# Linear attention: VectorE copies the second sweep's corner ahead of the sum of the keys' squares

## What is computed

```python
x = x + _L0_attn_ref(_layernorm(x), ...)
x = x + _L0_ffn_ref(_layernorm(x), ...)
x = x + _L1_attn_ref(_layernorm(x), ...)     # the gated delta rule
x = x + _L1_ffn_ref(_layernorm(x), ...)
```

```python
q = _l2norm(q) * Dk ** (-0.5); k = _l2norm(k)        # x * rsqrt(sum(x * x) + eps)
attn = -(einsum('bhcid,bhcjd->bhcij', k_beta, k) * decay_mask)   # strictly lower triangle
# rows corrected one after the other: the inverse of a unit triangular matrix
value_corrected = attn @ v_beta
...
out = inter + einsum('bhij,bhjd->bhid', intra, v_prime)
new_state = state * gel_c[..., None] + einsum('bhld,bhle->bhde', k_c * kd_c, v_prime)
```

## Time and profile before

| | us |
|---|---|
| median of 3 runs | 1651.46 |
| lowest and highest | 1650.98, 1653.03 |
| the profiled execution, its own time | 1658.11 |
| its span, first to last instruction | 1656.3 |
| first run of the loop with a next head, start of its ksum | 549.50 |
| last such run, start of its ksum | 1406.87 |
| TensorE busy over the span | 1406.0 (85%) |
| VectorE busy over the span | 1159.5 (70%) |

### The profile page before, as it was taken

The page is one execution under the profiler, slowest core; times in us unless marked ns, Lnnn a source line. Parts: engine busy times, 40 slices in busy tenths (PEclk is TensorE's granted clock), DMA queues, the critical chain, the costliest instruction groups (busy, mean ns, idle before and its releaser), DMA issues. The chain is left out here.

```text
span 1656.3 us, 38451 instructions
## 1 busy us (share of the span) xinstructions
PE 1406.0 (85%) x14366; PEld 1000.5 (60%) x14366; DVE 1159.5 (70%) x2384; ACT 827.7 (50%) x2173; POOL 784.9 (47%) x1112
## 2 busy tenths in 40 slices
PE   5987995596555989999999999999999999976575
PEld 2443344464423657677777777777777777764464
DVE  5888117573566787888888888888888888833623
ACT  2333982224033655666665665666666666632122
POOL 5101001487024366457567566566566656633443
PEclk9998998699776999999999999999999999977787
DMA  8200005282724454564654664655556556331883
GB/s 278 85 2 2 1 1 155 89 249 107 251 51 98 109 146 114 149 158 127 161 158 129 150 154 140 146 155 148 141 152 156 130 151 171 89 91 58 247 253 130
DMA packets 249433, 218.72 MB, mean 132 GB/s; under 512 B 88770, under 2 KB 224962, under 8 KB 247200
## 3 DMA queue, kind: packets, MB, share of 16 engines
q1 hardware_dynamic: 234992, 192.41, 43.1%
q0 software_dynamic: 5712, 15.60, 2.8%
q10 hardware_dynamic: 8544, 8.26, 1.6%
HBM read 133.85 MB, written 82.25 MB: 130 GB/s over the span
## 5 line engine op out<-in xcount | busy, mean ns | idle before, releaser
L1974 DVE SCALAR_TENSOR_TENSOR d_conv<-d_big,all_cw,d_conv 128x1023 f32<-128x1023 f32 (+2 forms) x192 | 245.3, 1278 | 46.2 <-ACT d_conv L2216 44.3
L1696 PE MATMUL d_big<-all_xn_t,all_w 128*128 128x512 f32 x512 | 251.8, 622 | 18.6 <-DVE d_conv L1974 11.8
L1696 PEld LDWEIGHTS d_big<-all_xn_t,all_w 128*128 128x128 f32 x512 | 93.7, 198 | 102.3 <-issue 89.0
L2450 POOL TENSOR_TENSOR d_y<-d_y,all_xn 128x256 f32<-128x256 f32 x128 | 97.8, 764 | 110.2 <-DVE d_y L2126 92.1
L2315 ACT COPY d_ys<-d_big 128x128 f32<-128x128 f32 x256 | 60.9, 266 | 178.3 <-PE d_big L1864 140.7
L1902 PE MATMUL d_big<-all_wo,d_yt 128*128 128x256 f32 x512 | 125.9, 391 | 13.8 <-DVE d_yt L2051 13.8
L1835 PE MATMUL d_big<-all_w,all_xn_t 128*128 128x256 f32 x512 | 124.3, 387 | 0.0
L2407 POOL TENSOR_TENSOR d_vs<-d_vs,d_sv 128x1024 f32<-128x1024 f32 x32 | 61.3, 1915 | 131.3 <-DMA d_vs<-turned_v_scratch 130.0
L1902 PEld LDWEIGHTS d_big<-all_wo,d_yt 128*128 128x128 f32 x512 | 97.1, 197 | 26.5 <-issue 14.3
L1835 PEld LDWEIGHTS d_big<-all_w,all_xn_t 128*128 128x128 f32 x512 | 94.5, 192 | 19.8 <-issue 8.8
L2025 DVE SCALAR_TENSOR_TENSOR d_AI<-d_big,d_b_col,d_decay 128x256 f32<-128x256 f32 x256 | 104.3, 474 | 1.4 <-PE d_big L1709 0.6
(11 more groups left out here) (451 smaller groups left out, 3552.8 us busy)
## 6 DMA issues: line engine op xcount, KB each, us to landing
turned_kq_scratch<-d_turned SPq DMA_DIRECT2D x32, 512.0 KB, 3.8
d_kq_tok<-turned_kq_scratch SPq DMA_DIRECT2D x128, 128.0 KB, 3.0
turned_v_scratch<-d_vs SPq DMA_DIRECT2D x16, 1024.0 KB, 4.1
d_vs<-turned_v_scratch SPq DMA_DIRECT2D x64, 256.0 KB, 5.6
grouped_y_scratch<-d_yx SPq DMA_DIRECT2D x32, 512.0 KB, 3.4
d_yx<-grouped_y_scratch SPq DMA_DIRECT2D x128, 128.0 KB, 3.2
all_w<-in_L_attn_W_qkvz SPq DMA_DIRECT2D x16, 768.0 KB
l_hold<-in_L_ffn_gate_up_proj SPq DMA_DIRECT2D x48, 192.0 KB, 3.3
```

The source lines that it names most:

```text
L1696: mm = pe.matmul(big[0][:, c, :], w_sb[par][:, k, n * DK:(n + 1) * DK], xn_t[:, k, c * 512:(c + 1) * 512], start=(k == 0), stop=(k == KD - 1))
L1974: dve.scalar_tensor_tensor(conv[:, sh:T], src[:, 0:T - sh], cw[:, bass.ds(g, 1), COLUMN_OF[j], 3 - sh], conv[:, sh:T], ALU.mult, ALU.add). ...
L2450: pool.tensor_tensor(part, part, zs[:, t, :], ALU.mult).then_inc(s["yg_s"], 1)
```

## The change

In VectorE's list of steps, `ksum` of the next head moves from ahead of `l1y` of this head to right behind it. Nothing else changes: the same instructions, the same waits, the same buffers. The first head's `ksum`, ahead of the loop, stays where it is.

```diff
@@ -1366,7 +1366,7 @@
 DVE_ORDER = steps_of("""
...
-    3; this l1p, l0x 2; next kq_turn 1; prev y_turn 0; next ksum; this l1y; next kb; this l2p; next products 0, products 1; this l2y; next products 2;
+    3; this l1p, l0x 2; next kq_turn 1; prev y_turn 0; this l1y; next ksum, kb; this l2p; next products 0, products 1; this l2y; next products 2;
```

## The result

The change made the kernel **3.2% slower**: the ratio of its times to those of the kernel before is 1.0316, 95% interval 1.027 to 1.0363 (median 1710.94 us, four runs between 1701.41 and 1731.22; the kernel before beside it 1651.22). The run of 1731.22 us was in a slower state of the chip and is not in the ratio. The profiled execution took 1706.88 us with a span of 1705.2, against 1658.11 and 1656.3: **48.9 us** more. The forecast was 29 more. So the sign came as forecast, and so did the mechanisms (the uncovered wait, the holds of the small steps, falls of TensorE's clock); the clock's term was much larger. The forecast's range was only just met: 1651.46 us times the ratio is 1703.6, and the range ended at 1704; the median itself, 1710.94, lies above it.

The account below looks back on a forecast made before the run. TensorE was taken as the bound, with l2p on its path. Uncovered wait 5 us, holds 18 and clock 6 made +29 on 1651.5: 1680.5 us, 1.8% slower; range 1656 to 1704.

Parts of the forecast that it names:

- the uncovered wait: VectorE's copy l1y waits for TensorE's corner product without the sum as cover: 0.50 us in the steady sweep, about 5 in all.
- What bounds the kernel: TensorE is busy 58.66 of 60 us of a steady sweep, so nearly every pause of it is paid in full.
- l2p's start as the price: A late l2p on VectorE is not made good again, so the change is priced by l2p's start alone.
- The holds: kb's small steps on VectorE fall into GpSimd's d_vs multiplies and end with them: 18 us over fifteen sweeps.
- the walk: The hold rule applied through fifteen sweeps, each keeping its multiplies' start: delays of 0.0 to 3.6 us, sum 23.
- the forecast's own check with all starts for all sweeps: Multiply starts drawn from all sweeps for all sweeps give about the same mean delay, 1.8 us in a steady one.
- The sum itself is not held: VectorE's sum starting inside a multiply in the second sweep: taken as 0, at most 1.2 us once or twice.
- The clock: TensorE's clock falls after long idles before L1782: two to three of four long ones, 6 us; bounds 0 and 23.
- the second one: Rival: multiplies 0.5 us earlier, holds 38 us and ten clock falls 26: +64, 1715 us; chance 0.08.
- the delay was not swallowed: Denies the rival that TensorE's products catch up after a late l2p: under 0.2%, some 1653 us; chance 0.04.
- nothing could be won: Denies the rival that the copy finds TensorE's product ready and l2p starts 0.41 us earlier: 1645.5 us; chance 0.04.

Follow-up runs that it names:

- experiment 7: experiment 5 with three unread 128x256 TensorE products added in its idle time, not in the last sweep; ratio 1.0162 to the kernel before.
- experiment 3: The changed kernel with l2p moved ahead of kb (l1y, ksum, l2p, kb, products); ratio 1.0496 to the kernel before, median 1739.05 us.
- experiment 8: The order of experiment 3, with GpSimd's multiplies waiting for kb as in experiment 1; ratio 1.0056 to the kernel before.
- experiment 1: The changed kernel with GpSimd's two d_vs multiplies waiting until kb's small steps are done; ratio 1.0012 to the kernel before, median 1658.23 us.
- experiment 2: The kernel before, old order, with GpSimd's multiplies waiting for kb as in experiment 1; ratio 0.9961, median 1649.39 us.
- experiment 6: The kernel before with the sum of the keys' squares made twice, GpSimd as it was; ratio 1.0249, median 1703.44 us.
- experiment 5: experiment 1 with the sum of the keys' squares made twice, the added one first and unread; ratio 1.0259 to the kernel before.
- experiment 4: The changed kernel with four unread 128x256 TensorE products ahead of its wait for l2p; ratio 1.0188 to the kernel before, median 1690.87 us.

## Why the prediction was right, and where it was not

**What bounds the kernel**: right. TensorE pays for each pause in full; experiment 7 shows a late VectorE passed on one for one (57.2 us from l2p to y_turn's end again, plus 4.8).

**l2p's start as the price**: right as a number here and wrong as a reason. In both orders the products start 0.73 us behind l2p, so either gives the same sum. Experiments 3 and 8 part them, and the products count.

**The uncovered wait**, 5 us: the mechanism was right and the size a little low. It measured 8: by experiments 1 and 2 (8), and by the trace after (26.6 less 18 of holds, 8.6). In a steady sweep it is 0.57 (l2p 3.68 us after y_turn's end in experiment 1, 3.11 in experiment 2) where the working had 0.50; it had put it at nothing in the first four sweeps.

**The holds**, 18 us: they measured 18. The rule (a first, third or fourth step that starts inside a multiply ends with it) held in every sweep (once both started at 1389.17, and VectorE went first), and the multiplies as a whole stayed where they had been: 2.4 to 3.7 us after y_turn's end from the third sweep on, but for one (4.6), against 2.4 to 3.9 before. But that each sweep keeps its own start was wrong, and which sweeps are delayed came out otherwise than the walk had it: l2p 2.9 us later in the fourth sweep (forecast 0.0), 3.7 in the eighth (0.2), 0.6 in the ninth (3.6). The eighth's multiply had started 3.9 us after y_turn's end and now did at 2.65; the ninth's went from 2.5 to 4.6. The sum held since it hangs on how the starts are spread, as the forecast's own check with all starts for all sweeps had said (1.8 us in a steady sweep); its agreement to the microsecond is luck. That the steps themselves are the victims and the multiplies the cause is shown by experiments 1, 2 and 6.

**The sum itself is not held**: right, though not for the reason first given there, that it has one source like the reciprocal: the first small step has one source too and is held. In the first sweep of the changed kernel the sum starts at 550.08, inside a multiply that ran from 548.85, and takes 1.22 us, as in all other sweeps. This is what the Trainium skill says, page "SBUF — State Buffer", section "Who interferes with whom"; there it also stands that GpSimd and VectorE share a port pair which one instruction takes to itself until it ends, and that an instruction with two SBUF inputs needs it, one with a single input outside the fast modes does not. The trace agrees: b_col with two inputs is held (up to 1.91 us for 0.17), the reciprocal with one is not (0.20, also at 809.96, which lies inside the multiply that began at 809.93). The first small step is a case that the number of inputs doesn't settle: it adds a constant to one SBUF input and is held all the same (1.85 us at the most), and no run here shows why it is. The runs show who is held and until when; that a shared port is the reason is the page's statement.

**The clock**, 6 us: this is the term that failed, in size. It measured 20.2. I had asked how many idles are above 2.29 us, the one of before that had brought the clock down, and took two to three of four. All twelve sweeps with a hold brought it down, those with 1.8 to 2.2 us of idling too, and experiment 5 shows it after 1.66, though only in eight cases of twelve. My upper bound, nine falls at 2.6 us, was 23. One fall of before was no basis for a lower limit on the idle time that matters; I should have taken the nine. Experiments 4 and 7 show that it is the idle time and not the delay: with TensorE kept busy 21 and 16 us come back by the ratios (10 and 12 by the traces' fourteen sweeps). In the terms of the rivals the result lies between the forecast and the second one (holds and clock in most sweeps, +64).

**The other rivals**: the delay was not swallowed, and in the changed kernel the copy never found TensorE's product ready (the wait before it is 0.3 us at the least, mostly 0.85), so nothing could be won.

Left open: when an idle brings the clock down, and what decides between a short and a long fall. Fifteen idles of 0.74 to 1.52 us in experiment 8 left it up; of twelve of 1.64 to 1.79 us in experiment 5 eight took it down and four did not; in experiment 4 one of 1.82 us directly behind 1.91 us of filler left it up. In the changed kernel and in experiment 3 idles of 1.80 us and more took it down every time. TensorE's stray pauses of 1.5 to 2.3 us among the corner products, which bring the clock down too (once each in experiments 1 and 2), aren't explained either.

## What to carry to other kernels

Moving a step costs more than its own wait: look at what the steps behind it will then run beside, and count VectorE's small instructions between SBUF tensors against GpSimd's long ones, which can turn 0.17 us into 1.9. If such a pair is close, order it with a semaphore (here worth 0.4% even in the kernel before, and 3% after the change). When TensorE is the bound and its pauses reach about one and a half microseconds, price the pause and the fall of its clock; here the second was about as large as the first (20 us beside 27, and 24 beside 17 in experiment 5).

## What was not expected of the hardware

The clock's falls have a length, and a price that grows with it. From sweep lengths of the changed kernel (l2p to l2p, less the next sweep's own distance from y_turn to l2p, less the 57.2 of an undisturbed one): 3.4 us at the lower level cost 1.0 us (six sweeps, 0.9 to 1.1), 6.8 us cost 3.1 and 3.4 (two; the first sweep, which has no y_turn and is shorter, is left out), 10.2 us cost 4.3 and 4.6 (two). An idle of 2.15 us was so followed by another 4.3 us of loss. The idles of 0.74 to 1.52 us in experiment 8, one in every sweep, brought no such loss.
